# Ring rows filled in the last attention slots, two small vectors loaded later, scaled rows turned between embedding groups

## What is computed

```python
def attention(x, emb):                    # x (4, 512, 512), emb (4, 1, 512), 16 heads of 32
    scale, shift = split(emb @ W_emb + b_emb)
    xn = rms_norm(x, g_norm) * (1 + scale) + shift
    q, k, v = heads(xn @ W_qkv)
    q, k = rms_norm(q, g_q), rms_norm(k, g_k)
    o = softmax(q @ k.T * 32 ** -0.5) @ v
    return o + o @ W_out

x = x + attention(x, cond_2048)
h = cond_2048                             # GRU over the 512 tokens, 4 batches
for t in range(512):
    gi = x[:, t] @ W_ih + b_ih
    gh = h @ W_hh + b_hh
    r, z = sigmoid(gi_r + gh_r), sigmoid(gi_z + gh_z)
    h = (1 - z) * tanh(gi_n + r * gh_n) + z * h
    out[:, t] = x[:, t] + h
```

## Time and profile before

| | |
|---|---|
| median of 3 runs | 2134.92 us (2133.56 to 2135.43) |
| the profiled execution | 2135.39 us, span 2133.6 us |
| granted TensorE clock | 1.000 |
| PE / PEld busy | 2104.6 / 1685.3 us |
| DVE / ACT / POOL busy | 1304.7 / 1130.5 / 188.3 us |
| first projection starts | 16.06 us |
| first step's matmuls start | 544.13 us |

### The profile page before, as it was taken

How to read it: one execution, slowest core, us unless ns; L and a number is a source line. 1 busy time by engine, 2 the same in 40 slices (tenths; PEclk the granted TensorE clock), 3 DMA queues, 4 the chain that set the end, 5 groups by cost and what they waited for, 6 DMA issues and landing times.

```text
span 2133.6 us, 130856 instructions
## 1 busy us (share of the span) xinstructions
PE 2104.6 (99%) x58097; PEld 1685.3 (79%) x58097; DVE 1304.7 (61%) x5004; ACT 1130.5 (53%) x5052; POOL 188.3 (9%) x227
## 2 busy tenths in 40 slices
PE   8999999999999999999999999999999999999998
PEld 5665666657988888888888888888888888888776
DVE  4776766666556566665666665666556565656555
ACT  5775766655444455445445454444545455444544
POOL 4443333331000000000000000000000000000000
PEclk9999999999999999999999999999999999999999
DMA  6000000004201000000000000000000000000000
GB/s 226 1 21 2 1 21 2 2 1 141 93 26 27 27 20 24 23 25 25 22 25 21 26 22 28 19 25 21 23 23 25 25 22 24 20 26 22 21 9 9
DMA packets 80575, 62.05 MB, mean 29 GB/s; under 512 B 43596, under 2 KB 75880, under 8 KB 80008
## 3 DMA queue, kind: packets, MB, share of 16 engines
q1 hardware_dynamic: 78960, 50.36, 7.9%
q0 software_dynamic: 528, 3.15, 0.4%
q10 hardware_dynamic: 520, 0.18, 0.0%
HBM read 29.80 MB, written 16.78 MB: 22 GB/s over the span
## 4 chain that ended last, share of the span: by engine, by line
PE 95%; DVE 2%; ACT 1%; issue 1%; POOL 1%; DMA 0%; SPq 0%; DVEq 0%; POOLq 0%
PE ps L688 64%; PE ps L400 7%; PE ps L593 7%; PE ps L494 6%; PE ps L614 3%; PE ps L630 3%; PE ps L464 2%; PE ps L478 1%; DVE nT L1062 1%; DVE xb L1073 1%; DVE ps L1067 1%; ACT xb L859 1%; PE ps L469 1%; DMA x1T<-in_L_cond_W_emb 0%; POOL qk_rs L373 0%
## 5 line engine op out<-in xcount | busy, mean ns | idle before, releaser
L688 PE MATMUL ps<-wqkv,xb 128*4 128x128 f32 x49152 | 1477.5, 273 | 13.2 <-DVE xb L1073 11.8
L688 PEld LDWEIGHTS ps<-wqkv,xb 128*4 128x4 f32 x49152 | 1226.7, 87 | 242.8 <-DVE xb L1073 209.9
L1062 DVE STREAM_TRANSPOSE rzT<-ps 128x128 f32<-128x128 f32 x512 | 162.8, 318 | 362.3 <-PE ps L688 362.3
L864 ACT ACTIVATE r_pair<-rzT 128x8 f32<-128x8 f32 x512 | 107.7, 210 | 482.6 <-DVE rzT L1062 482.6
L1073 DVE TENSOR_TENSOR_SCAN xb<-z_trip,xb 128x24 f32<-128x24 f32 x1024 | 212.9, 208 | 188.1 <-ACT xb L859 130.6
L859 ACT ACTIVATE xb<-ps 128x16 f32<-128x16 f32 x1024 | 190.0, 186 | 132.0 <-DVE ps L1067 121.5
L825 ACT ACTIVATE probs<-ps,negmax 128x512 f32<-128x512 f32 x256 | 173.2, 689 | 102.8 <-DVE negmax L995 102.7
L494 PE MATMUL ps<-wih,x1T 128*32 128x192 f32 x3392 | 223.1, 326 | 0.0
L871 ACT ACTIVATE z_trip<-znT 128x8 f32<-128x8 f32 x512 | 109.5, 214 | 182.3 <-DVE znT L1062 181.8
L593 PE MATMUL ps<-wqkv,xnT 128*128 128x384 f32 x512 | 204.4, 487 | 1.0 <-ACT xnT L771 1.0
L843 ACT ACTIVATE ps<-seeds 128x256 f32<-128x256 f32 x512 | 194.3, 380 | 0.0
(11 more groups left out here) (90 smaller groups left out, 1372.5 us busy)
## 6 DMA issues: line engine op xcount, KB each, us to landing
gi_spill<-gi_image SPq DMA_DIRECT2D x64, 192.0 KB, 2.3
seeds<-gi_spill SPq DMA_DIRECT2D x226, 32.0 KB
seeds<-gi_spill SPq DMA_DIRECT2D x282, 16.0 KB
seeds<-blank SPq DMA_DIRECT2D x10, 384.0 KB, 3.3
out<-xb SPq DMA_DIRECT2D x240, 16.0 KB
xb<-in_x SPq DMA_DIRECT2D x3, 1024.0 KB, 5.5
wih<-in_L_cond_W_ih SPq DMA_DIRECT2D x1, 3072.0 KB, 16.4
seeds<-blank SPq DMA_DIRECT2D x1, 3072.0 KB, 20.6
```

The costliest lines, as they stand in the source:

```text
L688: last = nc.tensor.matmul(ps[QD * j:QD * j + B, bank, 0:P], hist_flat[:, first:first + 3 * B - 2:3], weights, start=False, stop=False, ski ...
L1062: return nc.vector.transpose(into[:].rearrange("p (r k b s) -> p k r s b", r=4, k=blocks, b=B, s=2), ps[:, bank, first:first + QD * blocks])
```

## The change

The ring rows 16 to 35 are filled in three transfers: rows 16 to 21 when the last scores are made, rows 22 to 26 when the last probabilities are transposed, rows 27 to 35 when the last values, copies are done. `v_sb` moves behind `probs` so that the buffers come free in the ring's order. `spill(1, 0)` goes behind them. Wave 2 is fetched in steps 4 to 7, and the fills leave the steps. In the head, `g_q` and `g_k` are loaded from SP's queue between the two parts of W_qkv, and ScalarE scales `g_k` after its scaled rows; the embedding groups and the transposed chunks take turns on TensorE, chunk 3 in another bank; each quarter of the first projection waits for its own chunk.

```diff
--- before.py
+++ after.py
@@ -132,9 +132,9 @@
             xnT = attention_only.enter_context(nc.sbuf_tensor("xnT", [P, 2, KT, T], F32))
             xr = attention_only.enter_context(nc.sbuf_tensor("xr", [P, TT, D], F32))
             sq = attention_only.enter_context(nc.sbuf_tensor("sq", [P, 2, 2 * P], F32))
-            v_sb = attention_only.enter_context(nc.sbuf_tensor("v_sb", [P, G, TT, P], F32))
             qkT = attention_only.enter_context(nc.sbuf_tensor("qkT", [P, 2, 2, T], F32))
             probs = attention_only.enter_context(nc.sbuf_tensor("probs", [P, 4, T], F32))
+            v_sb = attention_only.enter_context(nc.sbuf_tensor("v_sb", [P, G, TT, P], F32))
             probsT = attention_only.enter_context(nc.sbuf_tensor("probsT", [P, 4, TT, P], F32))
             embT = sq[:, 0, :]
         seeds = sb("seeds", [P, RING, GCOL])
@@ -152,6 +152,7 @@
         LAST_GROUP = ALL_QUADS - TT
         GI0_SLOT, Y0_SLOT = ALL_TILES, LAST_GROUP + LAG + 1
         EARLY_RING = 2 * WAVE
+        SCORES_RING, HEADS_RING = EARLY_RING + 6, EARLY_RING + 11
 
         def piece_of(slot):
             b, u = divmod(slot, N_TILES)
@@ -167,6 +168,7 @@
         FULL_Y = KT * (B - 1)
 
         X_BANKS = (PO, PJ[0], PJ[1], PM)
+        XN_BANKS = (SC[0], SC[1], SC[2], PO)
         EMB_BANK, VECTORS_BANK = SC[3], SC[2]
         N_COND, N_BEMB, N_GN = B * KT, 2 * KT, KT
 
@@ -252,6 +254,8 @@
                 sp.dma_start(wemb[:, k, :], W_emb[P * k:P * k + P, :]).then_inc(ld_emb[k], 16)
             for a in range(3):
                 sp.dma_start(wqkv[:, :, D * a:D * a + P], nat(W_qkv)[:, :, D * a:D * a + P]).then_inc(ld_wqkv_first, 16)
+            sp.dma_start(g_row[:, 0, :], g_q.partition_broadcast(P)).then_inc(ld_g, 16)
+            sp.dma_start(g_row[:, 1, :], g_k.partition_broadcast(P)).then_inc(ld_g, 16)
             for a in range(3):
                 sp.dma_start(wqkv[:, :, D * a + P:D * a + D], nat(W_qkv)[:, :, D * a + P:D * a + D]).then_inc(ld_wqkv_rest, 16)
             sp.wait_ge(ld_wqkv_rest, 48)
@@ -302,23 +306,25 @@
                 fetch(sp, 0, 0, j)
             for j in range(4):
                 fetch(sp, 0, 1, j)
-            spill(1, 0)
+            sp.wait_ge(s["s_done"], 4 * ALL_QUADS)
+            fill(EARLY_RING, SCORES_RING, ld_blank_mid)
+            sp.wait_ge(s["pt_done"], 4 * ALL_QUADS)
+            sp.wait_ge(s["exp_done"], 4 * ALL_QUADS)
+            fill(SCORES_RING, HEADS_RING, ld_blank_rest)
             sp.wait_ge(s["pv_done"], ALL_QUADS)
             sp.wait_ge(s["ptev_act"], 2 * ALL_QUADS)
-            sp.wait_ge(s["exp_done"], 4 * ALL_QUADS)
+            fill(HEADS_RING, RING, ld_blank_rest)
+            spill(1, 0)
             for step in range(T):
                 m, u = divmod(step, BLK)
-                if 1 <= step <= 10:
+                if 4 <= step < 8:
                     sp.wait_ge(s["seeded"], step + 2)
-                    first = EARLY_RING + 2 * (step - 1)
-                    fill(first, first + 2, ld_blank_mid if step <= 4 else ld_blank_rest)
-                if 6 <= step < 10:
-                    if step == 6:
-                        sp.wait_ge(ld_blank_mid, 16 * 4)
-                    fetch(sp, 0, 2, step - 6)
+                    if step == 4:
+                        sp.wait_ge(ld_blank_mid, 16)
+                        sp.wait_ge(ld_blank_rest, 16 * 2)
+                    fetch(sp, 0, 2, step - 4)
                 if 12 <= step < 16:
-                    if step == 12:
-                        sp.wait_ge(ld_blank_rest, 16 * 6)
+                    sp.wait_ge(s["seeded"], step + 2)
                     fetch(sp, 0, 3, step - 12)
                 if step in fetch_steps:
                     n, due = fetch_steps[step]
@@ -415,22 +421,31 @@
 
             pe.wait_ge(s["cond_ready"], 1)
             pe.wait_ge(s["bank_zero"], 1)
-            for k in range(KT):
+            def emb_part(k):
                 pe.wait_ge(ld_emb[k], 16)
                 for j in range(4):
                     last = nc.tensor.matmul(ps[QD * j:QD * j + B, EMB_BANK, 0:2 * P], condT[:, k, :],
                                             wemb[:, k, :].rearrange("p (c j x) -> p c j x", c=2 * KT, j=4)[:, :, j, :],
                                             start=(k == 0), stop=(k == KT - 1), tile_position=(0, QD * j))
-            last.then_inc(s["emb_done"], 1)
-
-            for c in range(KT):
-                if SC[c] == EMB_BANK:
-                    pe.wait_ge(s["embT_done"], 1)
+                return last
+
+            def first_rows(c):
+                if XN_BANKS[c] == X_BANKS[0]:
+                    pe.wait_ge(s["xT_ready"], 1)
                 for t in range(TT):
                     if c == 0:
                         pe.wait_ge(s["xr_ready"], t + 1)
-                    last = transpose(ps[:, SC[c], P * t:P * t + P], xr[:, t, P * c:P * c + P])
+                    last = transpose(ps[:, XN_BANKS[c], P * t:P * t + P], xr[:, t, P * c:P * c + P])
                 last.then_inc(s["xn_ps"], 1)
+
+            emb_part(0)
+            first_rows(0)
+            emb_part(1)
+            first_rows(1)
+            emb_part(2)
+            first_rows(2)
+            first_rows(3)
+            emb_part(3).then_inc(s["emb_done"], 1)
             pe.wait_ge(ld_wqkv_first, 48)
 
             def await_piece(slot):
@@ -590,6 +605,8 @@
                 def project(k):
                     b, tile = divmod(n, N_TILES)
                     g, t = divmod(tile, TT)
+                    if n == 0:
+                        pe.wait_ge(s["xnT_act" if k % 2 else "xnT_dve"], k // 2 + 1)
                     return nc.tensor.matmul(ps[:, pj(n), 0:3 * P], xnT[:, b % 2, k, P * t:P * t + P],
                                             wqkv[:, k, :].rearrange("p (a g n) -> p a g n", a=3, g=G)[:, :, g, :],
                                             start=(k == 0), stop=(k == KT - 1))
@@ -639,7 +656,7 @@
                 if n < ALL_TILES:
                     if n == TT:
                         pe.wait_ge(ld_wqkv_rest, 48)
-                    if n % N_TILES == 0:
+                    if n % N_TILES == 0 and n > 0:
                         pe.wait_ge(s["xnT_dve"], 2 * (n // N_TILES) + 2)
                         pe.wait_ge(s["xnT_act"], 2 * (n // N_TILES) + 2)
                     if n >= 6:
@@ -750,8 +767,6 @@
             act.dma_start(vectors[0:N_COND, :], cond.rearrange("b (k p) -> (b k) p", p=P)).then_inc(ld_cond, 16)
             act.dma_start(vectors[N_COND:N_COND + N_BEMB, :], b_emb.rearrange("(c p) -> c p", p=P)).then_inc(ld_cond, 16)
             act.dma_start(vectors[N_COND + N_BEMB:N_COND + N_BEMB + N_GN, :], g_norm.rearrange("(c p) -> c p", p=P)).then_inc(ld_cond, 16)
-            act.dma_start(g_row[:, 0, :], g_q.partition_broadcast(P)).then_inc(ld_g, 16)
-            act.dma_start(g_row[:, 1, :], g_k.partition_broadcast(P)).then_inc(ld_g, 16)
 
             def sum_squares(part):
 
@@ -764,8 +779,6 @@
             sum_squares((0, 1))
             act.wait_ge(ld_x, 16)
             sum_squares((2, 3))
-            act.wait_ge(ld_g, 32)
-            nc.scalar.mul(g_row[:, 1], g_row[:, 1], DH ** 0.5).then_inc(s["gk_ready"], 1)
             def scaled_rows(b, c, bank):
                 act.wait_ge(s["xn_ps"], b * KT + c + 1)
                 nc.scalar.activation(xnT[:, b % 2, c, :], ps[:, bank, :], ACT.Identity,
@@ -782,7 +795,9 @@
                 raw_rows(0, c, X_BANKS[c])
             act.wait_ge(s["mod_ready"], 1)
             for c in (1, 3):
-                scaled_rows(0, c, SC[c])
+                scaled_rows(0, c, XN_BANKS[c])
+            act.wait_ge(ld_g, 32)
+            nc.scalar.mul(g_row[:, 1], g_row[:, 1], DH ** 0.5).then_inc(s["gk_ready"], 1)
             for slot in range(N_SLOTS):
                 j, i, m = slot - 1, slot - 2, slot - LAG
                 if 0 <= j < ALL_TILES:
```

## The result

The changed kernel takes **2144.39 us** (median of 8 runs, 2139.98 to 2149.67), against 2135.57 us for the kernel before (8 runs on the same chip, 2133.56 to 2140.25). The ratio is 1.0036, 95% interval 1.0026 to 1.0046: slower by about 7.7 us (the medians differ by 8.8), where 4.3 was the least that can be told. I had forecast 2136.7, a range that ended at 2140.0, and no change that can be told; all three were wrong. The profiled execution took 2144.68 us with a span of 2142.9, 9.3 us longer than before's.

A forecast was written before the change was run, and what follows sets the result against it. The prediction took TensorE to bound the kernel (95% of the span), so only its idle time counts. Head -0.4, steps -0.9 and hand-over +3.1 gave +1.8 us: 2136.7 us for the median, range 2132.9 to 2140.0.

The forecast's parts named there:

- Hand-over, the seeds: End of attention: ScalarE's fetches of quarters 2 and 3 of wave 0 can wait behind B at no cost.
- B: Hand-over fill of ring rows 22 to 26, 960 KB; data forecast to move from 538.75 to 541.75.
- C: Hand-over fill of ring rows 27 to 35, 1728 KB; data forecast right behind B, to 547.15.
- rival 3: Hand-over: ScalarE's small loads, or instruction packets, queue behind all of C; net +3.5 to +5.9, 2138.4 to 2140.8; chance 0.13.
- Hand-over, the instruction packets: Hand-over: instruction packets wait behind B and C; TensorE stands 1.8 and 1.3 us, sum 3.1 us lost.
- The 3072 KB fill: Attention, 474.4 to 493.2: an instruction packet delayed amid this fill cost nothing, since few instructions are used there.
- Head: Start of the kernel: first projection at 15.68 instead of 16.06, gain 0.4 us, from 0 to 0.95.
- the chain of groups and chunks: Head, TensorE: embedding groups at 0.55 and transposed chunks at 0.45 alternate, so emb_done comes 0.58 later, at 13.79.
- the move of the g loads: Head: g loads leaving ScalarE's queue for SP's were worth nothing, as the chain does not pass there.
- Steps 1 to 10: Recurrence: without the ten fills the 3.98 us step goes; gain 0.9 us, between 0.6 and 0.9.
- Range: Whole kernel: 2132.9 (packets take turns, head gain 0.95) to 2140.0 us.
- the forecast: Whole kernel: 2136.7 us (2135.9 to 2138.5), no change that can be told; chance 0.45.

The follow-up runs named there:

- the ring alone: The kernel before with only the ring's edits (three large fills, spill(1,0) and the fetches moved), head as before; ratio 1.0018 to the kernel before.
- one long fill: The kernel before with all twenty ring rows filled in one transfer of 3840 KB at step 1; ratio 1.0024 to the kernel before.
- the head alone: The kernel before with every head edit (g loads on SP, turned order, wait by quarter), ring as before; ratio 0.9999 to the kernel before.
- the seeds moved: The changed kernel with SP fetching all four quarters of wave 0 ahead of its fills, ScalarE none; ratio 1.0023 to the kernel before.
- half of the turn: The kernel before with the head's edits, but the last embedding group ahead of the transposes of chunks 2 and 3; ratio 0.9992 to the kernel before.
- the wait by quarter alone: The kernel before with only the quarter waits of the first projection; one execution, first projection at 15.21 against 16.06.
- one row per fill: Kernel before: g loads on SP, quarter waits, SP fetching all seeds, rows 16 to 21 filled early, 14 rows one per step; ratio 0.9988.
- no turning, and the seeds first: The kernel before with g loads on SP, quarter waits, old TensorE order, SP fetching all four seed quarters, fills as before; ratio 0.9995.

## Why the prediction was wrong

**Hand-over, the seeds: the step that failed.** I wrote "a turn behind B fits in that; nothing in the sum". The four loads did take their turn behind B, but C came on top of it, which I had put at nothing: their packets moved in three bunches from 543.7 to 549.7, and TensorE stood 3.37 us. In effect this is rival 3, at a chance of 0.13, and its price for the hand-over was near: 4.8 us, against 5.4 (first step at 551.35 instead of 544.23, of which 1.75 had come earlier). Its mechanism was only half right. It had the loads' data start behind all of C; they began when B had passed and took turns with C. That the two come out alike is in part luck: B and C moved more slowly (9.7 us) than the 8.4 that I took from one short fill, and the loads ended 0.5 us before C and not 1.5 behind it. Its landing of 548.6 was 2 us early mainly because B was issued 1.7 us later than I had it, at 539.28. I also read too much into the earlier trace rows. That queues take turns once both have begun is what happened under C; what a turn costs among fills of 40 and 72 rows per engine it doesn't say.

**Hand-over, the instruction packets.** The term was 1.8 us for the first and 1.3 for the second. The first is there with 1.48, or 1.9 with all by which the quarter ends late. The second was covered by the seeds' wait and came out as 2.73 when that was removed. The packets started at 543.95 and 550.15, where B's data had ended at 543.5 and C's at 550.3. So the mechanism was right, and the sum missed that the second stall and the wait for the seeds share time: the seeds' wait was the one to count last.

**Half clock after the wait: not in the sum.** An idle time of 3.4 to 3.9 us was followed by a granted clock of 0.50 in the changed kernel and in the runs with the ring alone and with one long fill, at a price of 1.2 us in after, and 2.7 in the ring's profile (1.2 in the first step, 1.5 in the second). Rival 3's price lacked this.

**The 3072 KB fill: not foreseen, and not the change's.** I had read the packet amid this fill and said that it cost nothing there. In after TensorE stands there 0.64 us and the slot comes 1.05 late. But the same stall is in the profile of the long fill (0.57), which is the kernel before, instruction for instruction, up to step 1, and in those with the head alone (0.53), the seeds moved (1.08), half of the turn (0.36), the wait by quarter alone (0.63) and one row per fill (0.55); the other five profiles, before's among them, don't have it. So 1 us of the profile's 9.3 comes and goes between executions. It does show that attention's thin code can be held up under a fill of 3072 KB, where I had inferred the opposite from a single profile.

**Head: the sign was wrong.** Forecast -0.4, in the profile +0.7. Two steps failed. First, the chain of groups and chunks: I took 0.55 and 0.45 a piece from a later stretch, but up to 11 us the pieces are slower. The first group takes 1.04, the first chunk 1.06, so that the second group starts at 11.47 and not at 10.72. Chunk 1 takes 0.59, chunks 2 and 3 1.03, and emb_done slipped 1.58 instead of 0.58. The weight loads (min/median/max ns, start in us) of the first chunk in after:

```profile
L406 PEld LDWEIGHTS ps<-ident,xr x4: 183/227/230, 10.5 to 11.0; 128*128 128x128 f32 x4
```

In before the same loads, at 13.1 and later, take 141. The windows print a granted clock of 1.00 in both places, but they print that too where the trace holds no record of the clock, and its first record, at 1.00, stands at 9.07 us in before and at 11.36 in after. In all twelve profiles the first record lies between 8.87 and 11.36 us, and the median 128x128 load of the head takes 230 ns ahead of it and 140 to 142 behind it. So TensorE was slower until then, which fits the lower level; the level itself isn't on record. That also sizes the loss. The three kernels with the whole turn start their first projection at 16.12, 16.19 and 16.76, with first records at 9.29, 10.05 and 11.36: some 0.6 of after's 0.7 goes with the late record and not with the edits, which leave 0.1. Second, I valued the move of the g loads at nothing since "the chain does not pass there". The chain passed through W_emb's landing, and the g loads held that up by 1.4 us and more. That they share the DMA engines with it was in the earlier trace rows for me to ask, and the half-idle window 6.0 to 8.5 was the place. Whether their descriptors or their 128-fold writes do it wasn't tried.

**Steps 1 to 10: right in the cause, less so in the size.** The 3.98 us step became 3.07, in after and, with halved fills, in the run with one row per fill (3.06). By itself that shows little, for with the head alone, where the fills are as before, the same step takes 3.06 too. There the twelfth takes 4.12 (DMA view, 580 to 581.9 us, with the last fill's data and a packet of q8 at 581.8; then TensorE's timeline):

```profile
DMA  0005988997999899599989997531100101001900
```

```profile
583.99 0.94 PE L702 MATMUL ps<-wqkv,xb 128*4 128x128 f32 x26 [0.70 <-issue]
```

In five of the six variants that keep the ten fills, steps of 3.84 to 4.39 us stand at the seventh step, the twelfth, or both; in the sixth (no turning, and the seeds first) the sixth and seventh take 3.39 and 3.57. Ahead of all these but one (the twelfth step of the wait by quarter alone) a packet starts within 0.15 us of the end of a fill's data. So which fill meets a packet changes with the timing before it, but these rows and the long fill show that one does and that TensorE then stands. In after's own profile two steps of 3.34 and 3.58 take back most of the 0.91.

**Range.** It ended at 2140.0, near rival 3's middle, though rival 3's own price went to 2140.8 and should have set the end. With 1.2 us for the clock and 0.1 to 0.7 lost in the head instead of 0.4 gained, rival 3 would have given 2140.1 to 2143.1. The point from which it decides was wrong as well: the 1.3 gained has to be added to the 4.3, not taken off, which needs a landing at 549.4 and not at 547.9. The earlier trace rows had packets due at 543 and 547 and the small loads stood between the same fills, so its chance deserved to be near that of the forecast.

## What to carry to other kernels

A bulk transfer issued ahead of small loads that the critical path needs soon, or over the time at which dense code fetches its next instructions, holds both up by microseconds; ask what else is due while it moves, and cut it into short pieces (here one row, 192 KB, per step, with which no step of the first fourteen took more than 3.56 us). When a row names a transfer as the releaser, ask whether the program waits for it there. When two waits overlap in time, price the later one and expect the other to come out when it is removed. Before turning an order to fill idle time, ask what ends that idle time: here two small loads elsewhere in the queues did, and moving them alone was worth more than the turn, which delayed the one result that the next stage waits for.

## What I had not expected of the hardware

- Two loads that copy a short vector to all partitions, on ScalarE's queue, kept the DMA engines at 0.52 busy and 150 GB/s from 6.0 to 8.5 us; with them issued later on SP's queue it was 1.03 and 419 GB/s.
- An instruction packet waited 4.3 us within one 3840 KB fill, and four small loads of 96 KB in all, under fills of 2688 KB, moved their first packet 3.3 us after the first issue (1.0 before) and needed 6.1 us from there (2.0 before). Of the ten fills of 384 KB one or two a profile held a packet up, and the step was 0.8 to 1.3 us longer.
- After 1.97 us of idle time the granted clock was 0.50 for over 3 us in the profiles of the head alone (16.9 to 20.3 us) and of the seeds ahead of the fills (16.1 to 19.5), and in the changed kernel's own profile, after the same 1.97 us, the projection still took its 7.98. After 2.00 us it fell in the run with one long fill, and after 2.73 it didn't with the seeds ahead of the fills. So what decides there isn't shown.
- The first record of the granted clock, at 1.00, comes between 8.87 and 11.36 us, and ahead of it the same 128x128 weight loads take 230 ns instead of 141. The windows print 1.00 for that stretch all the same.
